# State-space stage on one Trainium2 core: one full-width skip product for a pair of heads, and the scan products of the two heads in turn

## What is computed

```python
xdt = xh * dtc[..., None]
Y_diag = jnp.einsum('bcln,bcsn,bhcls,bcshp->bclhp', Cc, Bc, Lmat, xdt)
states = jnp.einsum('bcln,bhcl,bclhp->bchpn', Bc, decay_states, xdt)
...
Y_off = jnp.einsum('bcln,bchpn,bhcl->bclhp', Cc, prevs, jnp.exp(A_cum))
Y = (Y_diag + Y_off + xh * D[:, None]).reshape(Bsz, L, D_INNER)
Y = Y * jax.nn.silu(z)
Y = Y * jax.lax.rsqrt(jnp.mean(Y * Y, axis=-1, keepdims=True) + EPS) * norm_w
```

## Time and profile before

| | before |
|---|---|
| median of three executions | 1099.04 us |
| the profiled execution: its time | 1100.47 us |
| its span | 1098.7 us |
| PE busy (matmuls) | 973.8 us, 89% |
| DVE busy | 784.4 us, 71% |
| ScalarE (ACT) busy | 685.6 us, 62% |
| GpSimd (POOL) busy | 518.1 us, 47% |
| granted TensorE clock, mean | 0.946 |

### The profile page before, as it was taken

How to read it: one execution, slowest core, us unless ns; L and a number is a source line. 1 busy time by engine, 2 the same in 40 slices (tenths; PEclk the granted TensorE clock), 3 DMA queues, 4 the chain that set the end, 5 groups by cost and what they waited for, 6 DMA issues and landing times. The chain is left out here.

```text
span 1098.7 us, 23216 instructions
## 1 busy us (share of the span) xinstructions
PE 973.8 (89%) x6744; PEld 855.6 (78%) x6744; DVE 784.4 (71%) x2028; ACT 685.6 (62%) x1467; POOL 518.1 (47%) x512
## 2 busy tenths in 40 slices
PE   4999999999999578999999958863399999799997
PEld 3988998898899335766766847763299999799997
DVE  5788888888887568999999836998455555355553
ACT  4566656656665479888898638882255555355553
POOL 5233223322422017877778544577344444244454
PEclk9999999999999698999999969985599999899999
DMA  5221131122110032343233039634244443233331
GB/s 179 72 73 50 48 95 48 48 64 79 48 38 0 25 82 77 78 77 78 77 78 67 12 98 289 207 128 143 86 139 146 122 127 106 86 94 99 96 98 48
DMA packets 82408, 99.09 MB, mean 90 GB/s; under 512 B 9243, under 2 KB 68258, under 8 KB 82186
## 3 DMA queue, kind: packets, MB, share of 16 engines
q1 hardware_dynamic: 72122, 74.24, 24.9%
q0 software_dynamic: 8752, 21.25, 5.5%
q10 hardware_dynamic: 1440, 2.43, 0.6%
HBM read 72.26 MB, written 27.02 MB: 90 GB/s over the span
## 5 line engine op out<-in xcount | busy, mean ns | idle before, releaser
L1805 PE MATMUL e_p_y<-w,e_gT 128*128 (+1 forms) x852 | 118.3, 275 | 0.0
L1752 DVE TENSOR_TENSOR e_g<-e_sl,e_p_h 128x342 f32<-128x342 f32 x142 | 72.6, 511 | 63.9 <-ACT e_sl L1730 55.5
L1716 POOL DMA_INDIRECT sorted_scratch<-e_xg x71 | 69.0, 972 | 90.7 <-DVE e_xg L1762 87.7
L1714 POOL DMA_INDIRECT out<-e_xg x71 | 68.9, 970 | 87.1 <-DVE e_xg L1762 79.6
L1734 ACT ACTIVATE e_gT<-e_p_gx 128x384 f32<-128x384 f32 x142 | 69.6, 490 | 64.0 <-PE e_p_gx L1795 64.0
L1730 ACT ACTIVATE e_sl<-e_p_h 128x342 f32<-128x342 f32 x142 | 64.9, 457 | 69.7 <-PE e_p_h L89 69.7
L1805 PEld LDWEIGHTS e_p_y<-w,e_gT 128*128 128x128 f32 (+1 forms) x852 | 106.1, 192 | 0.4 <-issue 0.4
L87 PE MATMUL e_p_h<-w_hi,e_xT_hi 128*128 x284 | 104.7, 368 | 1.5 <-DVE e_g L1752 0.8
L1756 DVE TENSOR_TENSOR e_xT_lo<-e_p_gx,e_xT_hi 128x128 fp32r<-128x128 f32 x142 | 41.4, 292 | 86.4 <-ACT e_xT_hi L1738 86.0
L1009 DVE SCALAR_TENSOR_TENSOR m_c<-m_p_x,m_vecs,m_c 128x506 f32<-128x506 f32 (+2 forms) x144 | 95.5, 734 | 2.0 <-ACT m_c L873 1.8
L89 PE MATMUL e_p_h<-w_hi,e_xT_lo 128*128 x284 | 92.6, 326 | 0.0
(11 more groups left out here) (386 smaller groups left out, 3316.5 us busy)
## 6 DMA issues: line engine op xcount, KB each, us to landing
e_xg<-sorted_scratch SPq DMA_DIRECT2D x142, 130.0 KB, 2.1
m_cum<-cum_scratch SPq DMA_DIRECT2D x16, 1024.0 KB, 7.9
g_adjT<-in_adjT SPq DMA_DIRECT2D x16, 512.0 KB, 3.8
g_adj<-in_adj SPq DMA_DIRECT2D x16, 512.0 KB, 4.8
c_adjT<-in_adjT SPq DMA_DIRECT2D x16, 512.0 KB, 5.5
x_tokens<-in_x SPq DMA_DIRECT2D x16, 256.0 KB, 4.8
sorted_scratch<-nothing SPq DMA_DIRECT2D x2, 1040.0 KB
sorted_scratch<-nothing SPq DMA_DIRECT2D x12, 130.0 KB
```

Source lines behind the costliest of these rows:

```text
L1714: sent = pool.indirect_dma_start(out_dram, home, xg[:, b, RES:RES + P], None, bounds_check=NT * P - 1, oob_is_err=False)
L1716: sent = pool.indirect_dma_start(sorted_dram[1], home, xg[:, b], None, bounds_check=ROWS - 1, oob_is_err=False)
L1752: dve.tensor_tensor(g[:, i % D3], sl[:, i % 2], p_h3[i % 2][:, 0:HP], ALU.mult).then_inc(q["g_ready"], 1)
L1805: last = pe.matmul(p_y[d % 2][:, 0:P], gT[0:r, d % D3, k], w2k[:, bass.ts(e, P)], start=k == 0, stop=k == len(CH) - 1)
```

## The change

Only `scan` changes. For each sequence `g` and each pair of heads `k`, the skip product is now one matmul with all 128 columns of `skip[:, k]` as its stationary operand. Behind it come the first-chunk products of the two heads of the pair, then the second-chunk products of both. What is summed into each element of `p_to` stays the same. A scan had 24 matmuls, all 64 columns wide; it now has 20: 4 of 128 columns and 16 of 64.

```diff
-                    for h in range(HEADS):
-                        k, p0 = h // 2, h % 2 * HD
-                        hs = slice(h * HD, (h + 1) * HD)
-                        l0 = g * N
-                        pe.matmul(p_to[p0:p0 + HD, k, l0:l0 + N], skip[:, k, p0:p0 + HD], xs[:, v % 3, k, l0:l0 + N], start=True, stop=False)
-                        pe.matmul(p_to[p0:p0 + HD, k, l0:l0 + N], xdt[:, v % 2, 2 * g, hs], W[:, v % 2, g, h, 0:N], start=False, stop=False)
-                        last = pe.matmul(p_to[p0:p0 + HD, k, l0 + P:l0 + N], xdt[:, v % 2, 2 * g + 1, hs], W[:, v % 2, g, h, N:NB], start=False, stop=True)
+                    l0 = g * N
+                    for k in range(2):
+                        halves = [(p0, 2 * k + p0 // HD) for p0 in (0, HD)]
+                        pe.matmul(p_to[:, k, l0:l0 + N], skip[:, k], xs[:, v % 3, k, l0:l0 + N], start=True, stop=False)
+                        for p0, h in halves:
+                            pe.matmul(p_to[p0:p0 + HD, k, l0:l0 + N], xdt[:, v % 2, 2 * g, h * HD:(h + 1) * HD], W[:, v % 2, g, h, 0:N], start=False, stop=False)
+                        for p0, h in halves:
+                            last = pe.matmul(p_to[p0:p0 + HD, k, l0 + P:l0 + N], xdt[:, v % 2, 2 * g + 1, h * HD:(h + 1) * HD], W[:, v % 2, g, h, N:NB], start=False, stop=True)
```

## The result

| | before | after |
|---|---|---|
| median of nine executions each | 1099.71 us (1098.37 to 1102.80) | 1105.72 us (1103.88 to 1109.84) |
| ratio of times, 95% interval | | 1.0050 (1.0037 to 1.0063) |
| the profiled execution: time, span | 1100.47, 1098.7 us | 1104.62, 1102.8 us |
| granted TensorE clock, mean | 0.946 | 0.949 |

The kernel is slower by 6.0 us (4.1 to 6.9 by the interval), which is more than the 0.2% that a measurement can tell. The forecast was 8.8 us more, 1107.8, in a range of 1103.5 to 1111.5.

What follows compares the result with a forecast made beforehand. The ring of PE and DVE was taken to bound the state-space phase; scans 2 to 15 at 7.7 us, scan 0 at 0.74 and scan 1 at 0.37 make 8.8, so 1099.04 + 8.8 = 1107.8 us, range 1103.5 to 1111.5.

Steps and rivals of the forecast that it cites:

- What bounds the phase: State-space phase: the ring sets the pace; its step grows from 14.41 to 14.96 us, DVE's wait from 0.77 to 1.3.
- A border: Change of matmul width on PE empties the array and exposes weight loads: 0.145 us from 128 to 64 columns, 0.20 back.
- The heads start together: In a scan, a pair's two heads in turn start within 0.02 us, removing the second half's 0.49 us lateness.
- One scan, +0.55: A scan on PE takes 4.32 + 0.58 + 0.60 = 5.50 us against 4.95, 0.55 us longer.
- the ring: State-space loop: DVE's gate waits for PE's scan, PE's gated product for DVE's update; one turn is a 14.41 us step.
- Scan 0: First scan of the phase, starting out of a wait for ACT, so no entry is saved: 0.74 us longer.
- Scans 2 to 15: 14 x 0.55 = 7.7: Fourteen later scans of the state-space phase, each waited for, also the last: 0.55 us each, 7.7 us together.
- what follows is unchanged: After the barrier of all engines that ends the state-space phase, the later work was to stay the same.
- no border: Rival: width changes inside a scan neither empty the array nor show weights; scan 0.63 us shorter, 1089.5 us, chance 0.05.
- weights hidden: Rival: the array empties at width changes but weight loads go under that; 0.015 us per scan, 1099.3 us, chance 0.03.
- a lag: Rival: a pair's second head starts up to 0.49 us late; 2.51 us per scan, 40 in all, 1139 us, chance 0.04.
- Strict order: Rival: old scan's heads do not overlap, near 7.9 us; the change saves 2.4 us per scan, 1062 us, chance 0.01.

Runs made afterwards that it cites:

- narrow kernel: Kernel after, with eight 64-wide skip products per scan, each kind of product for a pair's two heads in turn: 1096.60 us, 0.9952 of the kernel before.
- POOL's squares moved: POOL's root and half_squares moved ahead of late and bias additions in its last turn: 1098.40 us on the kernel before, 1108.01 on the kernel after.
- last four scans alone: Kernel before with the new order in scans 12 to 15 only, the old order in the others: 1100.03 us, ratio 0.9986.
- head-by-head kernel: Kernel after, but behind each wide skip product first- and second-chunk products of one head, then of the other: 1108.04 us, 1.0065 of the kernel before.
- second profiles: One more profiled execution each of the unchanged kernels before and after: 1102.73 and 1107.32 us.

## Why the prediction was right, and by how much not

- **What bounds the phase**: right. The step is 14.98 us (14.96 forecast), the wait 1.34 (1.3), PE's wait for the update is as before.
- **A border**: right. 0.31 to the first 64-wide pass (0.30 forecast), its second pass 0.27 later, 0.20 to the next skip pass and 0.32 to its second one. The Trainium skill, "TensorEngine Tiling (Array Packing)", "Key Properties", says that a change of tiling mode drains the array; the trace agrees, with 0.09 us empty at each border and the second pass 0.055 or 0.105 later than usual.
- **The heads start together**: right, 0.007 us apart in the narrow kernel, and also where they need not have (0.013).
- **One scan, +0.55**: right, +0.57 on the ring. Scan 0 measured 0.76 (0.74 forecast), scan 1 0.24 (0.37). Scans 14 and 15 come out of waits like scan 0 and grew by 0.69 and 0.74, which I had put at 0.55.
- **The step that failed** is the last one of the sum: "Scans 2 to 15: 14 x 0.55 = 7.7; each is waited for, also the last", and with it "what follows is unchanged". The turn behind the loops, 15.84 or 18.10 us long before, was not read: in it PE already waited 1.80 us for POOL's squares, a wait that takes up a later PE, and the clock fell behind it; none of my rows was of it. With POOL's squares moved, the phase grew by 8.85, so the ring's sum holds where that wait is gone. That it meets 8.8 so closely is in part luck: the 11 steps and scans 14 and 15 gave 0.6 more than their terms, scan 1 and the turn (0.10 instead of 0.55) 0.6 less. Without the move the phase grew by 7.30 and 6.39 in the two pairs of profiles, and by 5.0 and 8.7 if they are paired crosswise, so how much the turn takes up differs from execution to execution. That the next phases gain 2 to 3 us is measured, in both profiles of the kernel after and with the last four scans alone, and goes with a shorter stretch at the lower clock; what sets that stretch is open.
- **The rivals**: no border (1089.5 us), weights hidden and a lag all fall by the rows above. Strict order falls by the head-by-head kernel: its second head starts 0.013 us behind the first, ahead of products issued earlier.

## What to carry to other kernels

Count borders between tile widths as work: a wide matmul that saves no stream time but stands between narrower ones costs two of them, here 0.35 us. Pair narrow matmuls on the two halves in turn, and keep the width the same or put the wide ones first (0.47 and 0.48 us a step gained here, against 0.57 lost). A steady step times its count is the sum only for as long as the ring lasts: read the turns behind the loop and the first microseconds of the next phase separately, since waits there took up part of the loss here. A gain can end at an engine that did not limit the step before: look which engine is nearly late, here POOL.

## What the chip showed that I had not expected

The old order starts its second head 0.49 us late with six passes of the first head issued ahead of it; head by head behind a wide product, with four passes ahead, it starts 0.013 us late. So the lag of the old order does not come from program order as such; how far PE looks ahead for work on the other half was not measured by itself.

PE's wait of 1.80 us for the squares went with 3.4 us at a granted clock of 0.50, one of 3.70 us with 6.8 (from 612.1, narrow kernel), one of 0.72 us with none; in the second profiles one of 2.5 us went with 6.8 (kernel before) and one of 1.1 us with 3.4 (kernel after, 626.7 to 630.1). The length of a wait alone does not tell, though: with POOL earlier the waits of 1.44 and 1.9 us for `m_CB` went with none. Where the clock did fall, the wait cost more than itself: in the kernel before 0.86 us on eight transposes and 0.54 on sixteen products, beside the 1.80.
